# A GNN layer and a mixture of experts: VectorE's steps regrouped, block numbers loaded quad by quad, TensorE's steps placed anew

## The reference

```python
x = x + gnn(layernorm(x), src, dst)     # summed = segment_sum(xn[src], dst); agg = summed / max(deg, 1)
                                        # out = concat([xn, agg]) @ weight; out = out / norm(out) + bias
x = x + ffn(layernorm(x))               # gate logits (8 experts), softmax, argmax; an expert takes its
                                        # first C tokens; relu(x @ w1 + b1) @ w2 + b2, times the gate value
```

## Time and profile before

| | |
|---|---|
| median of 3 runs | 1400.24 us (1398.0 to 1404.33) |
| the profiled execution | 1398.44 us |
| its span | 1396.6 us |
| busy: PE, DVE, ACT, POOL | 80%, 62%, 33%, 65% |
| mean granted TensorE clock | 0.973 |

### The profile page before, as it was taken

How to read it: one execution, slowest core, us unless ns; L and a number is a source line. 1 busy time by engine, 2 the same in 40 slices (tenths; PEclk the granted TensorE clock), 3 DMA queues, 4 the chain that set the end, 5 groups by cost and what they waited for, 6 DMA issues and landing times.

```text
span 1396.6 us, 29269 instructions
## 1 busy us (share of the span) xinstructions
PE 1120.8 (80%) x4989; PEld 820.2 (59%) x4990; DVE 868.0 (62%) x3856; ACT 464.5 (33%) x1360; POOL 907.4 (65%) x931
## 2 busy tenths in 40 slices
PE   1076766788889898989888898989898888887786
PEld 1054554566666666666666666666666666654454
DVE  8645454666666666666666666666666666665443
ACT  3511212233333333333333333333333333334342
POOL 3167676677777777777777777777777777731101
PEclk9999798999999999999999999999999999999999
DMA  7686878443444434343433434343434344321111
GB/s 246 199 269 206 249 226 243 148 127 116 131 123 123 130 118 133 115 132 114 128 115 112 121 110 121 110 126 110 125 110 121 114 113 120 113 75 43 47 38 35
DMA packets 113601, 183.38 MB, mean 131 GB/s; under 512 B 21419, under 2 KB 84448, under 8 KB 113584
## 3 DMA queue, kind: packets, MB, share of 16 engines
q0 software_dynamic: 43328, 109.52, 27.2%
q1 hardware_dynamic: 70256, 73.69, 17.6%
HBM read 155.29 MB, written 35.83 MB: 137 GB/s over the span
## 4 chain that ended last, share of the span: by engine, by line
DVE 29%; PE 27%; DVEq 20%; issue 18%; DMA 3%; ACT 2%; ACTq 0%; SPq 0%; POOLq 0%; POOL 0%
PE ps_q L726 14%; PE ps_h L792 7%; DVE sel L1037 6%; DVEq L1301 6%; PE ps_t L800 2%; PE ps_b L811 2%; DVE acc L1046 2%; DVEq L1108 2%; DVEq L894 2%; DMA b_b<-in_L_ffn_b 2%; DVEq L1037 1%; DVEq L1064 1%; DVE row L1150 1%; DVE idx L1033 1%; DVE bn L1156 1%
## 5 line engine op out<-in xcount | busy, mean ns | idle before, releaser
L461 POOL DMA_INDIRECT ring<-xn_d,idx x784 | 788.0, 1005 | 316.5 <-issue 171.5
L726 PE MATMUL ps_q<-ring,sel 128*128 128x257 f32 x1952 | 582.8, 405 | 151.2 <-DVE sel L1037 119.9
L726 PEld LDWEIGHTS ps_q<-ring,sel 128*128 128x128 f32 x1952 | 346.5, 195 | 291.5 <-issue 234.3
L1037 DVE SCALAR_TENSOR_TENSOR sel<-lane,block,dst_t 128x512 f32<-128x512 bf16 x245 | 184.3, 752 | 132.8 <-issue 76.6
L811 PE MATMUL ps_b<-w_sb,hid_t 128*128 x832 | 213.8, 385 | 16.1 <-ACT hid_t L626 16.1
L1046 DVE TENSOR_TENSOR acc<-acc,ps_q 128x257 f32 x245 | 103.2, 421 | 178.4 <-issue 166.9
L792 PE MATMUL ps_h<-w_sb,hid_t 128*128 x416 | 200.0, 608 | 6.2 <-ACT hid_t L594 6.2
L811 PEld LDWEIGHTS ps_b<-w_sb,hid_t 128*128 128x128 f32 x832 | 153.5, 190 | 49.0 <-issue 30.1
L621 ACT ACTIVATE hid<-ps_h 128x512 f32<-128x512 f32 x104 | 62.1, 597 | 190.4 <-PE ps_h L792 190.4
L626 ACT ACTIVATE hid_t<-ps_t,b_t 128x128 f32<-128x128 f32 x416 | 113.2, 383 | 31.5 <-PE ps_t L800 31.5
L792 PEld LDWEIGHTS ps_h<-w_sb,hid_t 128*128 128x128 f32 x416 | 75.5, 191 | 67.4 <-issue 65.2
(11 more groups left out here) (194 smaller groups left out, 1230.0 us busy)
## 6 DMA issues: line engine op xcount, KB each, us to landing
w_sb<-in_L_ffn_w SPq DMA_DIRECT2D x32, 512.0 KB, 9.7
ring<-xn_d,idx POOLq DMA_INDIRECT x784, 2.8
disp_d<-hid SPq DMA_DIRECT2D x8, 1040.0 KB, 7.9
xs<-disp_d SPq DMA_DIRECT2D x53, 130.0 KB
ys<-disp_d SPq DMA_DIRECT2D x53, 130.0 KB
b_b<-in_L_ffn_b SPq DMA_DIRECT2D x53, 128.0 KB
xb<-in_x SPq DMA_DIRECT2D x51, 128.0 KB
out<-row SPq DMA_DIRECT2D x51, 128.0 KB
```

The source lines that it names most:

```text
L461: pool.indirect_dma_start(ring[:, (k % 2) * TQ + j, 0:D], None, xn_d[:, :], bass.IndirectOffsetOnAxis(ap=idx[:, k * TQ + j:k * TQ + j + 1] ...
L726: mm = pe.matmul(ps[:, 0:AW], sel[:, s, j, :], ring[:, (k % 2) * TQ + j, 0:AW], start=(j == 0), stop=(j == TQ - 1), skip_group_check=True)
L1037: dve.scalar_tensor_tensor(out=sel[:, s, :, :], in0=lane[:, :].rearrange("p (j m) -> p j m", j=1).to_broadcast((P, TQ, P)), scalar=block0[ ...
```

## The change

- **Block numbers.** The eight registers become two (`ends_of`). VectorE loads the next quad's two numbers at the end of each `select_quad`, TensorE in the first entry of each quad's list. The load and the register moves of the trip go.
- **Indices.** VectorE's four small copies to `idx` become two on ScalarE (`gather_rows`), each for two quads, the second of them after the counts of the trip. GpSimd waits for them once in two quads.
- **Copies and arithmetic on ScalarE.** The send copy goes from VectorE to ScalarE, in `exponent`. `row_norm` gets four more one-element activations with drains between them, which replace VectorE's Newton step. The bias row is multiplied by the gate value on ScalarE (`out_bias`), so that `result` needs one step where it had two.
- **ScalarE's order.** `prepare_node(t + 1)` stands at the end of trip t, so ahead of the next trip's copy for the gate.
- **VectorE's order.** `route` has five rounds instead of nine and no longer waits for the exponent. `new_row`, `choose` and `finish_row` are one set of chains, between select 3 and the add that follows it; `result` stands alone.
- **TensorE's order.** The entries of `plan` move: cat transposes one quarter earlier, the linear's first half to the end of quad 0, up to the end of quad 1, the second hidden transposes to the end of quad 2, and in quad 3 the down steps come one quarter each, with the normalised row's transposes and the last down step at the end. The normalised row has a tile of its own, `xl`.

```diff
@@ ScalarE @@
             def row_norm(t):
...
-                rsqrt_start(sm[:, 2:3], sm[:, 0:1], sm[:, 1:2]).then_inc(norm_ready, 1)
+                rsqrt_start(sm[:, 2:3], sm[:, 0:1], sm[:, 1:2])
+                act.drain()
+                act.activation(sm[:, 3:4], sm[:, 0:1], ACT.Identity, scale=sm[:, 2:3])
+                act.drain()
+                act.activation(sm[:, 4:5], sm[:, 3:4], ACT.Identity, scale=sm[:, 2:3])
+                act.drain()
+                act.activation(sm[:, 5:6], sm[:, 4:5], ACT.Identity, scale=-0.5, bias=half3[:, :])
+                act.drain()
+                act.activation(sm[:, 6:7], sm[:, 5:6], ACT.Identity, scale=sm[:, 2:3]).then_inc(norm_ready, 1)
...
+            def out_bias(c):
+                act.wait_ge(ys_in, 32 * c)
+                act.activation(b2_b[:, :], b2_b[:, :], ACT.Identity, scale=ys[:, C_GATE:C_GATE + 1]
+                               ).then_inc(bias_ready, 1)
...
-            def trip(t, chunk=True):
+            def trip(t, chunk=True, next_known=None):
                 c = chunks(t)
-                act.load([blk], ntab[0:1, ds(t, 1)])
                 act.wait_ge(xl_ps, t + 1)
                 act.activation(cat_t[:, 0:KD, :], ps_a[:, 0:KD, :], ACT.Copy).then_inc(xlt_ready, 1)
-                prepare_node(t, act.snap(blk, min_val=0, max_val=NB - 2))
+                gather_rows(t, 1)
...
+                    out_bias(c)
                 exponent(t)
                 row_norm(t)
                 if chunk:
-                    hidden(c, e)
+                    hidden(c, 0)
+                act.wait_ge(count_ps, t + 1)
+                gather_rows(t + 1, 0)
+                if chunk:
+                    hidden(c, 1)
+                    relus(c, e)
                 next_row(t)
+                prepare_node(t + 1, next_known)
@@ TensorE @@
-                plan = [[steps((prev, gate), (chunk, load_expert)),
+                plan = [[steps((prev, gate), (chunk, load_expert), (quads, load_quad, 1)),
+                         steps((node, cat_transposes)),
+                         steps((chunk, xc_transposes)),
+                         steps((node, linear, 0))],
+                        [steps((node, linear, 1), (quads, load_quad, 2)),
                          steps(),
-                         steps((node, cat_transposes), (chunk, xc_transposes)),
-                         steps()],
-                        [steps((node, linear, 0)),
-                         steps((node, linear, 1)),
-                         steps((chunk, up, 0)),
-                         steps()],
-                        [steps((prev, counts), (chunk, up, 1), (quads, load_quads)),
+                         steps(),
+                         steps((chunk, up, 0))],
+                        [steps((prev, counts), (quads, load_quad, 3)),
+                         steps((chunk, up, 1)),
                          steps((chunk, hid_transposes, 0)),
-                         steps((chunk, hid_transposes, 1)),
-                         steps((chunk, down, (0, 1)))],
-                        [steps((chunk, down, (2, 3))),
+                         steps((chunk, hid_transposes, 1))],
+                        [steps((chunk, down, (0, 1)), (quads, load_quad, 4)),
+                         steps((chunk, down, (2, 3))),
                          steps((chunk, down, (4, 5))),
-                         steps((chunk, down, (6, 7))),
-                         steps((node, xl_transposes), (quads, turn_quads))]]
+                         steps((node, xl_transposes), (chunk, down, (6, 7)))]]
@@ VectorE @@
                 dve.wait_ge(visit_done, dve.snap(n) + 1)
                 select(q, k % 2, to)
+                dve.load(ends_of, qtab[0:1, ds(t * QS + k + 1, 1), :])
...
                 if quads:
-                    dve.load(next_regs, qtab[0:1, ds(t * QS + QS, QS), :])
                     dve.wait_ge(cat_ready, t + 1)
                     add_last(t, 0)
                     select_quad(t, 1)
-                chains(route(t) if prev else [], choose(t, whole=prev) if chunk else [],
-                       send_copy(t) if prev else [])
-                if quads:
+                    chains(route(t))
                     add_last(t, 1)
                     select_quad(t, 2)
-                chains(result(t, node) if chunk else [],
-                       ([nothing] if chunk else []) + finish_row(t) if prev else [])
-                if quads:
+                    if chunk:
+                        chains(result(t, node))
                     add_last(t, 2)
                     select_quad(t, 3)
-                    for now, then in zip(regs, next_regs):
-                        dve.reg_mov(now, then)
-                if node:
-                    new_row(t)
-                if quads:
+                    chains(new_row(t, known), choose(t) if chunk else [], [nothing] + finish_row(t))
                     add_last(t, 3)
-                if node:
                     normalise_row(t)
-                if quads:
                     select_quad(t + 1, 0)
-                if node and next_node:
                     prepare_node(t + 1, next_known)
```

More of the change, by code:

```diff
@@ L223, in gnn_moe_layer @@
         ys_in = sem("ys_in")
+        bias_ready = sem("bias_ready")
         xc_ready = sem("xc_ready")
@@ L654, in trip @@
                 if chunk:
-                    hidden(c, e)
+                    hidden(c, 0)
+                act.wait_ge(count_ps, t + 1)
+                gather_rows(t + 1, 0)
+                if chunk:
+                    hidden(c, 1)
+                    relus(c, e)
                 next_row(t)
-            with act.Fori(0, C0) as t:
+                prepare_node(t + 1, next_known)
+            prepare_node(0)
+            trip(0, chunk=False)
+            with act.Fori(1, C0) as t:
                 trip(t, chunk=False)
@@ L757, in load_expert, with load_quad @@
                     expert.append(pe.snap(code[1], min_val=0, max_val=EX - 1))
-                def load_quads():
-                    pe.load(next_regs, qtab[0:1, ds(t * QS + QS, QS), :])
-                def turn_quads():
-                    for now, then in zip(regs, next_regs):
-                        pe.reg_mov(now, then)
+                def load_quad(k):
+                    pe.load(ends_of, qtab[0:1, ds(t * QS + k, 1), :])
                 def cat_transposes():
@@ L1169, in normalise_row @@
                 dve.drain().then_inc(stat2_ready, 1)
-            def send_copy(t):
-                def copy():
-                    if not isinstance(t, int):
-                        dve.wait_ge(disp_out, 16 * t)
-                    dve.tensor_copy(sent[:, :], row[:, :])
-                return [nothing, copy]
             def route(t):
@@ L1295, in s7, with trip @@
                     dve.sem_inc(res_ready, 1)
-                return [s0, s1, s2, s3, s4, s5, s6, s7]
-            def trip(t, quads=True, node=True, prev=True, chunk=True, next_node=True, next_known=None):
+                return [s0, s2, s3, s4, s5, s6, s7]
+            def trip(t, known=None, quads=True, node=True, prev=True, chunk=True, next_node=True, next_known=None):
+                if known is None:
+                    known = dve.snap(blk, min_val=0, max_val=NB - 2)
                 if quads:
-                    dve.load(next_regs, qtab[0:1, ds(t * QS + QS, QS), :])
                     dve.wait_ge(cat_ready, t + 1)
@@ L1304, in trip @@
                     select_quad(t, 1)
[L1305 to L1307 removed]
+                    chains(route(t))
                     add_last(t, 1)
                     select_quad(t, 2)
[L1310 to L1312 removed]
+                    if chunk:
+                        chains(result(t, node))
                     add_last(t, 2)
                     select_quad(t, 3)
[L1315 to L1319 removed]
+                    chains(new_row(t, known), choose(t) if chunk else [], [nothing] + finish_row(t))
                     add_last(t, 3)
[L1321 removed]
                     normalise_row(t)
[L1323 removed]
                     select_quad(t + 1, 0)
[L1325 removed]
                     prepare_node(t + 1, next_known)
+                else:
+                    chains(route(t) if prev else [], choose(t, whole=prev) if chunk else [])
+                    chains(result(t, node) if chunk else [], finish_row(t) if prev else [])
+                    chains(new_row(t, known) if node else [])
+                    if node:
+                        normalise_row(t)
+                        if next_node:
+                            prepare_node(t + 1, next_known)
             dve.wait_ge(const_in, 16 * 4)
             prepare_node(0)
[L1330 removed]
+            dve.load(ends_of, qtab[0:1, 0:1, :])
             select_quad(dve.snap(n), 0)
@@ L1346, in _ @@
             dve.reg_add(t_reg, t_reg, 1)
-            trip(dve.snap(t_reg, min_val=TRIPS, max_val=TABW - 3), quads=False, next_node=False)
```

(1 more changed line is left out.)

166 lines of the change are left out of this document (84 added, 82 removed).

## The result

The changed kernel takes 1539.72 us (median of 4 runs, 1537.85 to 1545.42), the kernel before took 1399.12 beside it (4 runs, 1397.47 to 1404.33): a ratio of 1.1005, 95% interval 1.0962 to 1.1047. Forecast was 1470, slower; the time lies 70 us above that and above the range. The profiled execution of the changed kernel spans 1536.7 us. The experiments further down are eighteen runs of ten kernels, each run beside the kernel before; in six of them that kernel took 1402 or 1405 us, and these test the theory, while in the other twelve it took 1630 to 1661 us, and these are set apart.

A forecast was written before the change was run, and what follows sets the result against it. No engine is full; a ring of hand-offs bounds the trip, with a GpSimd floor of about 23.8 us. +56+18-6+2 = +70 on 1398.4 gives 1468.4, forecast as a median of 1470, range 1385 to 1515.

The forecast's parts named there:

- The ring: Circle of engine waits setting a chunk trip, counted from T, quad 2's last visit; trip 1.55 us longer, bounds +0.5 and +1.9.
- The ten rounds: VectorE's merged chain behind quad 3's select (new row, next chunk, slot): 4.55 us, bounds 4.2 to 5.0, against 3.05 before.
- small change: Unitemised remainder in TensorE's dense work from the visit behind the gate to the next T, put at 11.2 us.
- The term +56: 36 chunk trips with two selects in quad 3, each 1.55 us longer: +56 us (18 to 68).
- The two-register load: Register loads replacing the eight-register load on VectorE and TensorE: 0.52 us each, from 0.30 for one and 1.87 for eight.
- the clock's term: TensorE's half clock after a thin stretch: 0.5 us a trip on average, between nothing and 1.7; +18 us (0 to 61).
- The rival built on it, 1513: TensorE's clock falls in nearly every trip: 36 x (1.55+1.7) = 117 us more, total 1513; chance 0.10.
- Early trips: Eight trips without a chunk, 23.75 us each: long load goes, 22.9 each; -6 us (-16 to +3).
- Start, late trips and tail: Start gains 1, three late trips lose 2, tail +1 from the result's first step waiting; sum +2 us (-3 to +8).
- GpSimd decides: Faster rival: copy ready by about T+11, loads covered, GpSimd's 18 DMAs set trips at 23.4 to 23.8; 1370, chance 0.17.
- The ring barely changes: Rival: loads hidden behind the gate, chain at its lower bound; about 1405 us (1398 to 1420), chance 0.18.
- It doesn't do what it says: Rival: two-register loads cost as much as four or more, VectorE's turn no shorter; near 1510 us, chance 0.05.

The follow-up runs named there:

- the filler: Changed kernel plus nine useless matmuls in TensorE's idle time around the gate, in trips with quads; 1474.94 us against 1402.30 for the kernel before, ratio 1.0524.
- the order alone on the kernel before: Kernel before, with a separate tile for the normalised row and ScalarE preparing next nodes ahead of the gate's copy; 1409.88 us, ratio 1.006.
- the order undone: Changed kernel with ScalarE again copying the gate's input before preparing the nodes; 1402.21 us against 1405.09 for the kernel before, ratio 0.9978.
- the loads moved: Changed kernel with TensorE's expert and quad register loads moved from behind the gate to ahead of quad 0's first linear matmul; 1464.72 us, ratio 1.0451.
- the choosing undone: Changed kernel with the next chunk chosen beside the routing again, six rounds in the merged chain instead of ten; 1415.89 us, ratio 1.0103.
- all three undone: Changed kernel with ScalarE's copy first, TensorE's two loads ahead of the first linear matmul, choosing beside the routing; 1371.16 us against 1405.09, ratio 0.975.

## Why the prediction was right and wrong

**The ring was right, step by step.** Second select of quad 3: T+1.76 forecast, T+1.80 measured (645.87). Row steps 1.0 behind it: 0.87. The ten rounds and the 0.15 to the add, 4.70 forecast: 4.71 (646.74 to 651.45). Normalising at T+7.9: T+7.92. Quad 0's select at T+9.65: T+9.72. The gate at T+12.9: T+13.1. From release to the next visit 1.5: 1.40. From there to the next T 11.2: 11.49 with the filler. The terms listed for this one add to 11.49 (2.06+10.66-0.5-0.3-0.43), so the "small change" that brought it to 11.2 was wrong, and is about what the ring's term lacks. With the clock kept the interval would have been 24.05+1.55 in 36 of 41 trips; with the filler it measures 25.63, against 24.0 before. The term +56 measures +65. One wait had not been foreseen, that of quad 3's first down step for the reading of the counts: the forecast had quad 3 end at T+7.7 and TensorE idle 1.8 us ahead of the transposes; it idles 1.02 ahead of the down steps and 0.34 there. The transposes wait for the row either way, so this cost nothing. The row that orders this is ScalarE's timeline, the copy behind two activations; the row that prices it is the gate's idle time.

**The two-register load was right.** 0.52 was worked out from one and eight registers; the load lines of TensorE and VectorE give (ns, min/median/max):

```profile
L801 PEldq TENSOR_LOAD <-qtab x196: 516/521/2482, 68.7 to 1376.9; - x196
```

```profile
L1108 DVEq TENSOR_LOAD <-qtab x197: 503/509/2564, 66.9 to 1380.4; - x197
```

**The step that failed is the clock's term.** I took 0.5 us a trip, +18 us; it was 1.59 a trip, +64. The price of one fall was right: I had 3.4 us at half clock and 1.7 lost; 34 trips have 3.4 us and four have 6.8, 143 us in all, and 64 us lost in 38 trips are 1.7 each. Its frequency was wrong: 38 of 40 intervals. I had the row that spoke for it, the thin stretch followed by half clock, and the early trips at 0.87, and set against them that trips with gaps of 1 to 1.5 us had never lost the clock. But the length of one gap says little: the order alone on the kernel before loses the clock in 7 intervals with no gap over 0.94 us, the kernel before in none with gaps of 1.3. What differs is how close the gaps stand. From the end of quad 3 to quad 1's first visit the kernel before idles 0.77+1.32 = 2.1 of 5.6 us, with some 3 us of dense work between the two waits. The changed kernel puts the waits for the row, for the gate and for the loads close together: between T+9.2 and T+14.5 it idles 0.34+1.48+0.79 = 2.6 of 5.3 us, most of it in the last 2.9. That this closeness is what counts is read from these kernels; no run varied it alone. The thin stretch was in the forecast itself ("some 2 us of matmuls"), and the average of 0.5 us between never and always had no row behind it. The Trainium skill, page "TensorE: Matmul & The Clock Gate", Part 1, that lack of activity and not load halves the clock, is borne out: nine matmuls more gave 65 us back. The rival built on it, 1513, had a chance of 0.10 and should have been the forecast; the time lies 27 us above even that, by the ring, the early trips and the tail.

**Early trips** were to gain 6 us and lost 5.5. With the order undone they take 192.4 (192.8 before), with the loads moved 192.6, with the filler 194.7, with the choosing undone 198.6; the order alone on the kernel before takes 197.7. So of the 5.5, 3.6 go with the clock (0.83 granted against 0.87), and either order or loads undone brings them all back. The 6 us never came: the best, with all three undone, is 191.3. Why, no run shows; the forecast had started from 23.75 us a trip, where the table has 24.1.

**Start, late trips and tail** were to add 2, and add 6.1 (-1.9+4.0+4.0). In the tail the result's first step now waits for ScalarE's bias step:

```profile
DVE b_b L1288 <- ACT b_b L622: 40.4, 8, 7.4
```

Before, it waited in the same eight slots 31.7 us for the transfer itself and once 3.7 for TensorE, 35.4 in all. That is 5.0 us more, 0.6 a slot as I had it, but not evenly: the first slot waits 7.4 instead of 3.7, the other seven some 0.2 more each. So the 4.0 us of the tail are nearly all in that first slot, and the others cost next to nothing, as forecast. Why the first waits so much longer no run isolates; the five variants of the changed kernel keep a tail of 109 to 111 us, and the order alone on the kernel before has 104.5.

**The sum again.** Ring +65 (56), clock +64 (18), early +5.5 (-6), start, late and tail +6 (2): +140, against +70.

**The rivals.** GpSimd decides: not in this kernel; it is full once the three parts are undone, at 1371, and the rival's 1370 was for just that, the copy early and the loads covered, though with the ten rounds left in place. The ring barely changes: no, the loads behind the gate cost 0.94 and the order 1.8 (25.63-23.84). It doesn't do what it says: it does; VectorE has 3237 instructions and 786.9 us of work, where it had 3856 and 868.0, and its loads cost what they should. The clock in nearly every trip: yes, in 38 of 40.

## What to carry to other kernels

When a change makes an engine's turn shorter but a stretch of it longer, follow the stretch: here VectorE lost a good deal of work and the trip grew, since the step that was moved ahead of a copy on another engine waits for what was lengthened. Count TensorE's idle time between two dense stretches as one amount; if several waits are brought together there and the profile shows even one half-clock stretch behind a stretch like it, work out the time with a fall in every trip and with none, and say which you expect and why; half of the trips, as with the loads moved, is a third outcome, and an average stands for none of them. And matmuls of no use in the idle time are a cheap test: they tell the clock's price from that of the waits.

## What was not expected of the hardware

The granted clock can alternate: with the loads moved, intervals of 25.0 and 26.7 us follow one another in one loop of equal work, half clock in 20 of 40. Over the kernels with the filler left out it is 0, 0, 0, 6, 7, 20 and 38 intervals of 40. So a program may stand just where the clock goes, and there a saving of 0.94 us on one link was worth 1.81.

A fall doesn't cost the same everywhere either: 1.7 us an interval in the changed kernel and its variants, 1.0 with the order alone on the kernel before, at the same 3.4 us of half clock.
